# First expert layer of a two-block model: gates stored beside the tokens and applied in the expert's output copy, combination statistics made on ScalarE, separate scratch for the two halves of batch 0

## The reference, cut to what matters

```python
def top2_dispatch(x, Wg, C):          # x: 1024 tokens of one of 4 groups, C = 86
    gates = softmax(x @ Wg)           # 24 experts
    ... # idx1, idx2: the two best; loc: place of the token in its expert's queue
    m1 = m1 * (loc1 < C); m2 = m2 * (loc2 < C)      # over capacity: dropped
    g1, g2 = (g1 / denom, g2 / denom)
    return combine, dispatch

def moe_apply(x, combine, dispatch, W, b):
    disp = einsum('sec,sd->ecd', dispatch, x)        # gather
    h = einsum('ecd,edf->ecf', disp, W) + b[:, None, :]
    return einsum('sec,ecf->sf', combine, h)         # weigh and gather back

def per_group(xf, lw, lb):
    h = moe_apply(xf, combine, dispatch, W1, b1)     # 128 -> 512
    h = relu(layer_norm(h, lw, lb))
    return moe_apply(h, combine, dispatch, W2, b2)   # 512 -> 128
```

## Time and profile before

| | us |
|---|---|
| median of 3 runs | 1452.51 |
| lowest, highest | 1450.52, 1453.23 |
| the profiled execution | 1453.28 |
| its span in the profile | 1451.5 |
| VectorE busy in the span | 1220.0 |
| TensorE busy | 1271.4 |
| ScalarE busy | 866.9 |
| POOL busy | 668.7 |

### The profile page before, as it was taken

The page is one execution under the profiler, slowest core; times in us unless marked ns, Lnnn a source line. Parts: engine busy times, 40 slices in busy tenths (PEclk is TensorE's granted clock), DMA queues, the critical chain, the costliest instruction groups (busy, mean ns, idle before and its releaser), DMA issues. The chain is left out here.

```text
span 1451.5 us, 21439 instructions
## 1 busy us (share of the span) xinstructions
PE 1271.4 (88%) x7260; PEld 884.6 (61%) x7260; DVE 1220.0 (84%) x2474; ACT 866.9 (60%) x2066; POOL 668.7 (46%) x632
## 2 busy tenths in 40 slices
PE   6888888887888875899999798689999999999997
PEld 5444444443443434788888676467766777777775
DVE  6857999998999999999999578687898855568876
ACT  5466757665797885465654547756545454544462
POOL 0026555604489965673653675519640043146300
PEclk9888999998989886899999899799999999999999
DMA  7002545545244431454553621000002044212200
GB/s 254 1 11 75 144 135 138 139 125 162 72 125 128 131 96 55 124 154 125 153 147 91 233 55 41 22 20 26 1 2 58 3 108 131 59 34 48 30 25 35
DMA packets 75763, 127.56 MB, mean 88 GB/s; under 512 B 11374, under 2 KB 38350, under 8 KB 75046
## 3 DMA queue, kind: packets, MB, share of 16 engines
q1 hardware_dynamic: 56198, 75.30, 17.4%
q0 software_dynamic: 19456, 50.88, 13.4%
HBM read 85.77 MB, written 40.37 MB: 87 GB/s over the span
## 5 line engine op out<-in xcount | busy, mean ns | idle before, releaser
L795 DVE TENSOR_TENSOR_SCAN sc_st<-sc_dA,sc_st 128x1024 f32<-128x1024 f32 x128 | 287.2, 2284 | 0.0
L2354 DVE COPY at_pT<-at_p_t 128x512 f32<-128x512 f32 (+1 forms) x192 | 108.8, 599 | 105.1 <-PE at_p_t L2131 104.9
L580 ACT ACTIVATE sc_dA<-sc_dt,g_state 128x511 f32<-128x511 f32 x256 | 169.1, 711 | 6.6 <-DVE sc_st L795 5.3
L777 DVE TENSOR_TENSOR sc_st<-sc_st,sc_p_bc 128x1024 f32<-128x1024 f32 x128 | 155.3, 1214 | 16.9 <-PE sc_p_bc L637 16.8
L767 DVE TENSOR_TENSOR sc_st<-sc_u,sc_p_bc 128x1024 f32<-128x1024 f32 x128 | 154.6, 1209 | 7.8 <-PE sc_p_y L668 5.3
L1444 POOL DMA_INDIRECT g_state<-r_scratch,moe_tab x96 | 120.7, 1258 | 86.2 <-PE e_bank L1541 58.9
L2227 ACT ACTIVATE at_pr<-at_pr,at_nmx 128x512 f32<-128x512 f32 (+3 forms) x256 | 140.1, 551 | 23.3 <-DVE at_nmx L2313 23.2
L1404 POOL DMA_INDIRECT g_state<-xn_scratch,moe_tab x88 | 108.0, 1227 | 98.6 <-PE e_bank L1480 48.5
L637 PE MATMUL sc_p_bc<-sc_bc,mamba_sel 96*128 96x512 bf16 x256 | 104.5, 410 | 55.7 <-DVE sc_st L767 51.7
L2111 PE MATMUL at_p_s<-g_xT,at_qT 128*128 128x512 f32 (+3 forms) x512 | 149.4, 435 | 0.0
L668 PEld LDWEIGHTS sc_p_y<-g_ident,sc_st 128*128 128x128 f32 x1024 | 124.9, 146 | 27.1 <-issue 14.8
(11 more groups left out here) (342 smaller groups left out, 2743.0 us busy)
## 6 DMA issues: line engine op xcount, KB each, us to landing
y_scratch<-g_state SPq DMA_DIRECT2D x24, 768.0 KB, 5.3
g_state<-W SPq DMA_DIRECT2D x48, 256.0 KB, 5.5
r_scratch<-g_state SPq DMA_DIRECT2D x16, 512.0 KB, 3.7
y_scratch<-g_state SPq DMA_DIRECT2D x24, 192.0 KB, 2.7
xn_scratch<-g_state SPq DMA_DIRECT2D x16, 256.0 KB, 3.7
g_state<-x SPq DMA_DIRECT2D x4, 512.0 KB, 7.1
g_state<-xn_scratch SPq DMA_DIRECT2D x8, 256.0 KB, 5.7
g_state<-x SPq DMA_DIRECT2D x1, 2048.0 KB, 13.0
```

What stands on the lines that cost most here:

```text
L580: ins = nc.scalar.activation(dA[:, m % 4, j, 1:L], dt[:, b % 2, h, 1:L], ACT.Exp, scale=negA[:, h, 2 * q + j:2 * q + j + 1])
L777: nc.vector.tensor_tensor(states, states, p_bc[:, k % 3, :].unsqueeze(1).broadcast_to([P, HALF, L]), ALU.mult).then_inc(row_used, 1)
L795: nc.vector.tensor_tensor_scan(st[:, m % RS, :, :].rearrange("p a b -> p (a b)"), dA[:, m % 4, :, :].rearrange("p a b -> p (a b)"), st[:, ...
L2354: v.tensor_copy(pT[:, n % 2, part, 0:cols], p_t[:, PT_BANK[part], 0:cols]).then_inc(pT_ready, 1)
```

## The change

Three things. First, the dense gates `ex` are stored to DRAM behind each token's row (rows of XW = 152 numbers instead of 128), so that the gathered rows bring them along; ScalarE's copy of an expert's product takes the gate as its scale, the stored rows are then weighted, and the combination sums them by products with the identity. Dropped tokens had a gate of zero; now their back address is one spare row of zeros behind the others (NO_ROW), which SP stores in the front stage. A buffer of gathered rows is now free only after the expert's last output copy. Second, the statistics of the combination are made by ScalarE: the copy to `hb` also sums its row, a small instruction makes the negative mean, and a Square with that shift sums the squares; `diagonals` and VectorE's part are gone. Third, `logs` and `lost` have a part for each half of batch 0, and `scalar_logs(1)` no longer waits for `u_ready`.

```diff
@@ FirstBatch
-        self.logs = scratch.sb("logs", [P, 2, L])
-        self.lost = scratch.sb("lost", [P, L])
+        self.logs = scratch.sb("logs", [P, HALF, 2, L])
+        self.lost = scratch.sb("lost", [P, HALF, L])
@@ scalar_logs
-        if h:
-            act.wait_ge(self.u_ready, 1)
-        else:
+        if h == 0:
             act.wait_ge(self.bc_done, 1)
@@ front_stage, sync
-                sp.dma_start(xn_dram[:, tiles(b), :], xn_rows[:, tiles(b), :]).then_inc(stored, 16)
+                sp.dma_start(xn_dram[:, tiles(b), 0:D], xn_rows[:, tiles(b), :]).then_inc(stored, 16)
...
+            sp.wait_ge(zeroed, 1)
+            for rows in spare_rows:
+                sp.dma_start(rows, zero_rows[:, 0:rows.shape[1]]).then_inc(zeros_stored, 16)
+            sp.wait_ge(routing.g_ready, 1)
+            sp.dma_start(xn_dram[:, :, D:XW], routing.ex[:, :, :]).then_inc(gates_stored, 16)
+            sp.wait_ge(zeros_stored, 16 * len(spare_rows))
+            sp.wait_ge(gates_stored, 16)
@@ front_stage, gpsimd
             pool.wait_ge(stored, 16 * B)
+            pool.wait_ge(turned, B)
+            nc.gpsimd.memset(zero_rows, 0.0).then_inc(zeroed, 1)
             pool.wait_ge(routing.tab_ready, 1)
+            pool.wait_ge(gates_stored, 16)
@@ Moe0Experts.pool, gather_x
             if e >= 4:
-                pool.wait_ge(self.piece_made, 5 * (e - 4) + 1)
+                pool.wait_ge(self.piece_read, 5 * (e - 3))
@@ Moe0Experts.tensor
-                    pe.wait_ge(self.diag_ready, t + 1)
                     for k in range(2):
-                        ins = nc.tensor.matmul(bank[:, t % 2, :], self.diag[:, t % 2, k, :], self.yk[:, t % 4, k, :],
+                        ins = nc.tensor.matmul(bank[:, t % 2, :], w["ident"], self.yk[:, t % 4, k, :],
                                                start=False, stop=(k == 1))
@@ Moe0Experts.scalar
-                nc.scalar.activation(self.out1[:, e % 2, h, :], bank[0:CP, k % 2, :], ACT.Copy).then_inc(
-                    self.piece_read, 1)
+                nc.scalar.activation(self.out1[:, e % 2, h, :], bank[0:CP, k % 2, :], ACT.Copy,
+                                     scale=self.xg[:, e % 4, h, D + e:D + e + 1]).then_inc(self.piece_read, 1)
...
-            nc.scalar.activation(less, self.mv[:, t, 0], ACT.Copy, scale=-1.0)
...
                     if t >= 4:
                         act.wait_ge(self.centred, t - 3)
-                        act.wait_ge(self.var_ready, t - 3)
-                    nc.scalar.activation(self.hb[:, t % 4, :], bank[:, t % 2, :], ACT.Copy).then_inc(
-                        self.combined, 1)
+                    nc.scalar.activation(self.hb[:, t % 4, :], bank[:, t % 2, :], ACT.Identity,
+                                         accum_out=self.total[:, t:t + 1]).then_inc(self.combined, 1)
                     next(root, None)
-                    diagonals(t + 2)
+                    act.wait_ge(self.combined, t + 1)
+                    nc.scalar.activation(self.stats[:, t, 2:3], self.total[:, t:t + 1], ACT.Copy,
+                                         scale=-1.0 / HID).then_inc(self.mean_ready, 1)
                     next(root, None)
+                    act.wait_ge(self.mean_ready, t + 1)
+                    nc.scalar.activation(self.squares[:, :], self.hb[:, t % 4, :], ACT.Square,
+                                         bias=self.stats[:, t, 2:3],
+                                         accum_out=self.square[:, t:t + 1]).then_inc(self.var_ready, 1)
@@ Moe0Experts.vector
-                    dve.wait_ge(self.combined, t + 1)
-                    link(v.bn_stats(self.stats[:, t, :], self.hb[:, t % 4, :]))
-                    v.bn_aggr(self.mv[:, t, :], self.stats[:, t, :]).then_inc(self.var_ready, 1)
@@ Moe0Output.sync, load_rows
-            sp.dma_start(self.xn_rows[:, t, :], self.xn_dram[:, t, :]).then_inc(self.xn_in[b], 16)
+            sp.dma_start(self.xn_rows[:, t, :], self.xn_dram[:, t, 0:D]).then_inc(self.xn_in[b], 16)
```

More of the change, by code:

```diff
@@ L39 @@
 CP = 96
+XW = D + E0
+NO_ROW = HG * E0 * CP
 E1, C1 = 128, 32
@@ L1267, in vector @@
         link(ins)
-        link(v.tensor_copy(r.back[:, :, :], rows[:, :, :]))
+        link(v.scalar_tensor_tensor(out=rows[:, :, :], in0=rows[:, :, :], scalar=-float(NO_ROW),
+                                    in1=valid[:, :, :], op0=ALU.add, op1=ALU.mult))
+        link(v.tensor_scalar(r.back[:, :, :], rows[:, :, :], float(NO_ROW), None, ALU.add))
         link(v.tensor_tensor(g[:, :, :], g[:, :, :], valid[:, :, :], ALU.mult))
@@ L1479, in turn @@
             for g in range(HG):
-                ins = nc.tensor.transpose(bank[:, k % 2, g * CP:(g + 1) * CP], self.xg[:, e % 4, g, :],
+                ins = nc.tensor.transpose(bank[:, k % 2, g * CP:(g + 1) * CP], self.xg[:, e % 4, g, 0:D],
                                           w["ident"][0:CP, 0:CP])
@@ L1571, in scalar @@
             yield
-        def diagonals(t):
-            if t < NT:
-                if t >= 2:
-                    act.wait_ge(self.biased, t - 1)
-                for k in range(2):
-                    ins = nc.scalar.activation(self.diag[:, t % 2, k, :], self.w["ident"], ACT.Copy,
-                                               scale=self.r.wk[:, k, t:t + 1])
-                ins.then_inc(self.diag_ready, 1)
         def refine(n):
@@ L1617, in refine @@
             ins.then_inc(self.scale_ready, 1)
-        diagonals(0)
-        diagonals(1)
         act.wait_ge(self.eps_set, 1)
@@ L1682, in vector @@
         v.memset(self.eps[:, 1:2], 1.5).then_inc(self.eps_set, 1)
-        yield from [None] * (DVE_SLOTS * (E0 + 1))
-        for u in range(self.UNITS + 4):
-            if 1 <= u <= self.UNITS:
-                for t in range(2 * u - 2, 2 * u):
-                    dve.wait_ge(self.combined, t + 1)
-                    link(v.bn_stats(self.stats[:, t, :], self.hb[:, t % 4, :]))
-                    v.bn_aggr(self.mv[:, t, :], self.stats[:, t, :]).then_inc(self.var_ready, 1)
-            yield
-            yield
+        yield
 class Moe0Output:
```

63 lines of the change are left out of this document (36 added, 27 removed).

## The result

The changed kernel takes 1441.33 us (median of 6, 1437.01 to 1446.21); the kernel before, run beside it, 1450.4 (6 runs, 1449.68 to 1453.23). The ratio is 0.9935, with a 95% interval of 0.9917 to 0.9954: faster by 0.5 to 0.8%. Forecast were 1435 us, within 1424 to 1447, and faster.

The account below looks back on a forecast made before the run. POOL was taken to pace eleven units of the combination, VectorE (94% busy) just behind. 1453.3 - 6.5 - 8.1 - 4.4 + 0.5 + 0.5 = 1435.3, stated as 1435 us; 1427 to 1444 (0.62), 8 in 10 within 1424 to 1447.

Parts of the forecast that it names:

- the three pairs ahead of the first weigh: Combination's start: three statistics pairs on VectorE's path before POOL's first weigh, 1.61 us each, are saved; 4.8 us.
- second rival: Combination: ScalarE becomes the bound, the pace becomes 12.8 us a unit, total 1444 us; chance 0.13.
- fourth rival: Front and combination: the removed wait is only replaced by another and the phase gives nothing, total 1446 us; chance 0.08.
- Front, -6.5: Front stage: without the wait for u_ready PE goes on 5.2 us earlier, plus some clock back; 5.2 to 8.3, taken 6.5.
- The gates' store, 72 ns a piece: Front's store of 4096 gate pieces: 72 ns each, 18.4 us, landing at 97.0, covered with 1 us to spare.
- third rival: Front: gates land late, delaying POOL's gathers; 1467 us at 200 ns a piece; chance 0.10 including another stall.
- First expert layer, +0.5: First layer's experts: scale operand adds 90 ns to each of ScalarE's 96 PSUM copies, mostly off the path; 0 to 2 us.
- Outside POOL's pace, five pairs, -8.1: Combination: three statistics pairs ahead of the first weigh and two after 524.20 leave VectorE's path, 5 x 1.61 us.
- Inside the pace, 11 x 0.4 = -4.4: Combination's eleven POOL-paced units: shifted scans delay gathers less, 12.4 to 12.0 us a unit; bounds -9.4 to +4.4.
- ScalarE's floor of 11.5 us a unit: Combination's ten units: statistics add 10 us to ScalarE, about 115 of 123.96, and POOL's pace cannot fall below that.
- The signs named: Trace signs: first weigh about 11 us earlier, ten units 115 to 128, VectorE idle about 20, ScalarE's POOL wait below 10.
- Output stage, +0.5: Output stage: tokens read in pieces of 512 bytes instead of 2 KB; 0 to 2 us, taken 0.5.

Follow-up runs that it names:

- own_scratch: Kernel before with only separate scratch for batch 0's two halves, so ScalarE does not wait for u_ready: 1443.4 us, ratio 0.9954; repeated: 1445.11 us, 0.9958.
- vector_stats: Changed kernel with the combination's statistics (bn_stats, bn_aggr) on VectorE again: 1447.2 us, ratio 0.9975.
- gates_four_times: Changed kernel with the gates stored four times, one after the other, before POOL may gather: 1443.69 us, ratio 0.9944.
- vector_bias: Changed kernel with the addition of ln_b moved from POOL to VectorE, full result kept: 1438.88 us, ratio 0.9916.
- after: The changed kernel with the whole change, against the kernel before: 1441.33 us, ratio 0.9935.
- after_again: The changed kernel run once more, unaltered: 1442.47 us, ratio 0.9929.
- late_relu: Changed kernel with ScalarE's ReLU moved behind its unit's two normalisations and two decays, about 2.8 us later: 1442.68 us, ratio 0.9939.
- shared_scratch: Changed kernel with the scratch shared again and the wait for u_ready back, so without the front's part: 1447.93 us, ratio 0.9983.
- before: The kernel before, without the change, the reference for all ratios: 1450.4 us run beside the changed kernel, ratio 1.
- no_bias: Changed kernel without the addition of ln_b, POOL's second tensor operation a unit, so the result is not shifted: 1421.15 us, ratio 0.9803.

## Why the prediction was right, and where it was off

*The sign and the range* hold: 1441.3 in 1424 to 1447, faster. The forecast was 17.5 us below the median shown then, and the gain is 9.1. The missing 8.4 are two terms of the combination, 3.5 and 5.9, less the 1.0 of costs that did not show. Of the 12.5 us forecast for the combination 3.1 came. The number fell into the range because the front was right, and so were the three pairs ahead of the first weigh. By number the result lies nearer to the second and the fourth rival (1444, 1446) than to the forecast, but not by their mechanisms.

*Front, -6.5.* Right: -6.7 and -6.1 us by the ratios of the two own_scratch series, PE going on at 69.06 for 69.3. The first scan came 6.3 and 4.9 us earlier in their profiles. What made it right was the step that PE has the routing product ahead of the one that waits, so that 5.2 us are gained and not 7.7. The fourth rival, that the wait is only replaced, is out.

*The gates' store, 72 ns a piece.* The size was off by a factor of seven, 10.7 ns measured, and the row it came from has pieces fifteen times as large. At half of that, my lower bound, it was far too dear still. The store landed in 5.4 us and not in 21, POOL's first gather was at 81.3 and not at 97, and the margin was at least 14 us, not 1. It changed nothing in the sum, but the third rival is out: four such stores did not move the first scan.

*First expert layer, +0.5.* Not told apart in this stretch: from the first scan to the first weigh vector_stats, which has the scale operand, takes 269.3, and the kernel before 269.8. Over the whole execution the travelling gates cost some 3 us (vector_stats against own_scratch), more than the 0.5 here and the 0.5 of the output stage together; where is open. ScalarE's copy did go from 590 to 680 ns, as forecast, from the page after:

```profile
L1584 ACT ACTIVATE g_state<-e_bank,g_state 96x512 f32<-96x512 f32 x96 | 65.0, 680 | 62.1 <-PE e_bank L1513 60.3
```

*Outside POOL's pace, five pairs, -8.1.* The three pairs ahead of the first weigh: 4.6 for 4.8. The two behind the twelfth: nothing that can be told. Twelve to sixteen took 42.1 to 43.6 us with the statistics on VectorE and 39.8 to 44.7 in the changed kernel and those with all of its parts. The step from "POOL is no longer the pace" to VectorE as the pace failed there: with the pair gone, VectorE waits for PE's row. In the changed kernel:

```profile
514.40 1.22 DVE L793 TENSOR_TENSOR sc_st<-sc_st,sc_p_bc 128x1024 f32<-128x1024 f32 x1 [4.06 <-PE sc_p_bc L653]
515.54 4.47 DVE L811 TENSOR_TENSOR_SCAN sc_st<-sc_dA,sc_st 128x1024 f32<-128x1024 f32 x2
520.84 1.22 DVE L783 TENSOR_TENSOR sc_st<-sc_u,sc_p_bc 128x1024 f32<-128x1024 f32 x1 [0.84 <-PE sc_p_y L684]
```

In the kernel before, the first of these waits is 1.58 us and the second is not there: 3.3 us more of waiting now, for the 3.2 of the two pairs. PE is late because the product ahead of that row waits for POOL's gather, and it runs at the lower level:

```profile
510.15 3.78 PE L1532 MATMUL e_bank<-g_state,g_ident 128*128 128x512 f32 x4 [1.68 <-DMA g_state<-y_scratch,moe_back]
513.73 0.63 PE L653 MATMUL sc_p_bc<-sc_bc,mamba_sel 96*128 96x512 bf16 x1
```

So POOL's pace reaches one step further than its last full unit. In gates_four_times the same two waits of VectorE are 4.30 and 4.22 us, with a granted clock of 0.50 from 515 to 527 and four such products in 3.78 us twice, where vector_bias has 1.98 at the upper level. These 3.6 us of waiting are the difference between the two profiles' 44.65 and 41.02; what spreads the others was not followed.

*Inside the pace, 11 x 0.4 = -4.4.* This term failed, within its bounds (-9.4 to +4.4): the eleven units take +1.5 us (+0.9 in the first, 12.87 for 11.97, and +0.6 for the ten from the means of the five profiles of after, after_again, late_relu, gates_four_times and shared_scratch, 125.6, and of the four of before, both own_scratch and vector_stats, 124.9). Without own_scratch's 127.54 the mean of the others is 124.0, and the eleven units take +2.4. The step that failed is the one on the phase: "a scan pair begins, relative to POOL's gathers, earlier and overlaps the weigh more and the gathers less". The scans did come earlier, but they moved mostly from one gather to another. In the kernel before, nine of the ten units have an undisturbed first gather and the delay on later ones (0.98, 2.70, 1.87 and 0.95 us behind 415.31, say). In the changed kernel five have it on the first two (2.79, 1.84, 0.95 and 0.95 behind 438.22), which costs the same. The forty gathers take 62.6 us here against 63.7, and 62.0 to 66.8 in the five profiles of the changed kernel and its parts against 62.2 to 64.4 in the four others: nothing saved. In the first unit the shift even costs: gathers of 2.82, 1.85, 0.95 and 0.95 us where 0.98, 0.95, 1.85 and 1.88 stood, which is its +0.9. And in four of the five profiles one scan pair of the ten meets POOL's addition, and both become longer:

```profile
L1456 POOL TENSOR_TENSOR g_state<-g_state,moe_ln_b 128x1024 f32<-128x1024 f32 x10 | 25.5, 2554 | 0.8
```

The mean is 2.35 us without such a meeting. So the ten units of this profile are 1.6 us longer by +2.0 for one addition, +0.7 of POOL's waits for VectorE and -1.1 for the gathers. At 412.13, shown above, it took 4.38 us, and beside it:

```profile
412.09 6.58 DVE L811 TENSOR_TENSOR_SCAN sc_st<-sc_dA,sc_st 128x1024 f32<-128x1024 f32 x2
```

Two scans take 4.47 us alone. A scan pair and POOL's addition that meet cost 2.1 and 2.0 us, about the length of one instruction of the other. The Trainium skill ("SBUF — State Buffer", on the shared port pair) says just that, an exclusive lock for a whole instruction; the prediction cited it and had worked out by it that the pace stays at 12.4 but for a shift of phase. That was the better forecast than my 12.0: the units came to 12.56. I had counted what the overlap saves on gathers, and neither that the next gather pays it again nor what it costs the weigh.

*ScalarE's floor of 11.5 us a unit.* Too high by 0.5 to 0.8: no_bias runs at 10.68 with ScalarE full, and in the changed kernel ScalarE is busy 109.66 us in ten units, 10.97 each. It rose by 4.8 us in ten units, not 10. A tile's added work is shorter than the 1.15 us of the forecast, from ScalarE's timeline in the changed kernel:

```profile
394.18 0.19 ACT L1655 ACTIVATION_READ_ACCUMULATOR g_state<-e_bank 128x1 f32 x1
394.27 0.19 ACT L1603 ACTIVATE e_rstd<-e_rstd 128x2 f32<-128x2 f32 x1
394.40 0.20 ACT L1659 ACTIVATE e_stats<-e_total 128x1 f32<-128x1 f32 x1
394.51 0.19 ACT L1606 ACTIVATE e_stats<-e_rstd 128x2 f32<-128x2 f32 x1
394.64 0.72 ACT L1663 ACTIVATE e_squares<-g_state,e_stats 128x512 f32<-128x512 f32 x1
395.26 0.19 ACT L1663 ACTIVATION_READ_ACCUMULATOR e_squares<-g_state,e_stats 128x1 f32 x1
```

The 0.34 of the forecast for the mean and two waits had no row behind it. Start to start it is 0.09 for the sum's readout, 0.11 for the mean, 0.62 for the Square and about 0.09 for its readout: 0.91. The small steps of the root stand in the gaps where the two waits for its own result would have been. The second rival, ScalarE as the bound, is out for this kernel: 13.8 us of its time is still wait for POOL. The rule beside it in the Trainium skill ("ScalarE: Activation LUTs", "Rules for kernel authors": additions and products to VectorE), read on the statistics, which it does not name, would have kept them on VectorE. Here ScalarE was the better place for them: vector_stats is 5 to 7 us behind.

*The signs named.* VectorE's idle time in the ten units is 21.3 us, as forecast (20), and they take 125.6, within the 115 to 128. ScalarE's wait for POOL, forecast below 10, is 13.8: ScalarE has less to do than I had reckoned. The first weigh, forecast about 11 us earlier, came 16.5 earlier in the first profile and 9.5 in the second (378.74); the difference is mostly the 6.0 us at the first scan.

*Output stage, +0.5.* From the sixteenth weigh to the end of the span: 885.25 before, 884.8 and 884.6 after. Nothing, where single profiles spread by some microseconds (881.9 and 883.4 in the two of own_scratch).

Sum, against the run beside it: 1450.4 - 6.4 (front, the mean of both) - 4.6 + 1.5 + 0 = 1440.9, and 1441.3 was measured. The terms are single profiles and means of few, each good to a microsecond or two, so that they meet within 0.4 is in part luck.

## What to carry to other kernels

Ask of each stage whose queue has no gap, and price the stage only by what leaves that queue: 25 us of VectorE's work were worth 5 to 7 here, and 2.36 us of POOL's a unit were worth 20. When work is moved off the pacing engine, look at which engine then stands in order behind a wait for it, and move that wait too: the same addition on VectorE brought 2 to 4 us with ScalarE's ReLU in its old place, and with the ReLU 2.8 us later 10 to 12 (against late_relu on the same chip), where the ReLU's move alone brought nothing. Take the price of many small DMA pieces from a row with small pieces, or leave it unbounded from below.
